# Attention with residual layer norm, one core: a second high-part copy moved to another round, the first input and the query weights loaded in pieces

## What is computed

```
q, k, v = x @ Wq.T, x @ Wk.T, x @ Wv.T + bv
a = softmax(q k.T * 384**-0.5 + adj)        # per graph and head; rows that are all 0 give 0
o = (a @ v) @ Wo.T + bo
out = layernorm(x + o)
```

## Time and profile before

| | |
|---|---|
| median of 3 runs | 1248.02 us (1247.92 to 1248.37) |
| profiled execution | 1248.19 us, its span 1246.4 us |
| TensorE matmul (PE) | 1218.8 us busy, 98% |
| TensorE weight load (PEld) | 1057.3 us, 85% |
| VectorE (DVE) | 1054.4 us, 85% |
| ScalarE (ACT) | 1017.0 us, 82% |
| GpSimd (POOL) | 866.7 us, 70% |

### The profile page before, as it was taken

One profiled execution on the slowest core, in us unless ns is written; L12 is line 12 of the kernel. 1 busy time (PEld: TensorE's weight loads), 2 busy tenths in 40 slices (PEclk: granted clock), 3 DMA queues, 4 the chain that ended last, 5 costly groups with the idle time before them and its releaser, 6 DMA issues.

```text
span 1246.4 us, 34374 instructions
## 1 busy us (share of the span) xinstructions
PE 1218.8 (98%) x11796; PEld 1057.3 (85%) x11796; DVE 1054.4 (85%) x5094; ACT 1017.0 (82%) x4007; POOL 866.7 (70%) x775
## 2 busy tenths in 40 slices
PE   8999999999999999999999999999999999999996
PEld 7888888888888888888888888888888888888885
DVE  5788888888888888888888888888888888888986
ACT  6888888888888878888887888788888888887874
POOL 1777777677677777777776777677777767776774
PEclk9999999999999999999999999999999999999999
DMA  6022211222121222112221212221122212122100
GB/s 232 22 72 86 79 55 54 82 75 80 56 77 61 72 86 80 54 54 83 74 79 61 80 55 71 86 79 54 58 83 71 80 62 79 54 71 86 54 28 26
DMA packets 58895, 88.85 MB, mean 71 GB/s; under 512 B 3680, under 2 KB 54624, under 8 KB 58720
## 3 DMA queue, kind: packets, MB, share of 16 engines
q1 hardware_dynamic: 58720, 86.65, 21.4%
HBM read 61.47 MB, written 25.17 MB: 70 GB/s over the span
## 4 chain that ended last, share of the span: by engine, by line
PE 77%; ACT 19%; DVE 2%; issue 1%; POOL 1%; DMA 0%; POOLq 0%; SPq 0%; DVEq 0%
PE turn_bank L208 17%; PE turn_bank L210 17%; PE turn_bank L209 17%; PE pT_bank L256 12%; ACT probs L496 11%; PE score_bank L244 9%; PE turn_bank L268 6%; ACT pT L503 4%; ACT qkT L484 2%; ACT xT_hi L472 1%; DVE neg_a L624 0%; DVE out_sb L688 0%; DMA xT_raw<-xT_dram 0%; POOL inv_std L779 0%; POOL probs L772 0%
## 5 line engine op out<-in xcount | busy, mean ns | idle before, releaser
L496 ACT ACTIVATE probs<-neg_a,neg_max 128x128 f32<-128x128 f32 x1536 | 596.1, 397 | 3.7 <-DVE neg_max L624 3.5
L772 POOL TENSOR_TENSOR probs<-probs,row_scale 128x768 f32<-128x768 f32 x256 | 376.7, 1471 | 199.8 <-DVE row_scale L652 199.8
L765 POOL TENSOR_TENSOR fold<-neg_a 128x384 f32<-128x384 f32 x256 | 282.9, 1105 | 124.5 <-DVE neg_max L624 124.4
L624 DVE CUSTOM_DVE_ANT_0 neg_a<-score_bank,adj_sb 128x128 f32<-128x128 f32 x1536 | 333.4, 287 | 0.1
L503 ACT ACTIVATE pT<-pT_bank 128x384 f32<-128x384 f32 x512 | 220.7, 484 | 102.9 <-PE pT_bank L256 102.8
L496 ACT ACTIVATION_READ_ACCUMULATOR probs<-neg_a,neg_max 128x1 f32 x1536 | 302.5, 197 | 0.0
L208 PE MATMUL turn_bank<-xT_hi,w_hi 128*128 128x512 f32 (+1 forms) x594 | 240.9, 406 | 2.3 <-DVE w_lo L606 2.3
L210 PE MATMUL turn_bank<-xT_hi,w_lo 128*128 128x512 f32 (+1 forms) x594 | 231.7, 390 | 0.0
L209 PE MATMUL turn_bank<-xT_lo,w_hi 128*128 128x512 f32 (+1 forms) x594 | 230.6, 388 | 0.0
L256 PE MATMUL pT_bank<-ident,probs 128*128 128x128 f32 x1536 | 217.1, 278 | 0.3 <-ACT pT L503 0.3
L256 PEld LDWEIGHTS pT_bank<-ident,probs 128*128 128x128 f32 x1536 | 173.8, 141 | 21.1 <-issue 1.1
(11 more groups left out here) (39 smaller groups left out, 1961.9 us busy)
## 6 DMA issues: line engine op xcount, KB each, us to landing
xT_raw<-xT_dram SPq DMA_DIRECT2D x32, 768.0 KB, 4.7
x_sb<-x_dram SPq DMA_DIRECT2D x32, 768.0 KB, 4.7
out_dram<-out_sb SPq DMA_DIRECT2D x128, 192.0 KB, 1.9
adj_sb<-adj_dram SPq DMA_DIRECT2D x32, 256.0 KB, 3.2
w_raw<-wq_t_dram SPq DMA_DIRECT2D x1, 576.0 KB, 5.7
w_raw<-wk_t_dram SPq DMA_DIRECT2D x1, 576.0 KB, 6.8
w_raw<-wv_t_dram SPq DMA_DIRECT2D x1, 576.0 KB, 7.8
w_raw<-wo_t_dram SPq DMA_DIRECT2D x1, 576.0 KB, 8.4
```

Of the source, the lines that this page charges most:

```text
L496: last = nc.scalar.activation(probs[t % 2][:, u, :], neg_a[t % 2][:, u, :], ACT.Exp, bias=neg_max[t % 2][:, u:u + 1], scale=-1.0, accum_ou ...
L624: last = nc.vector.tensor_tensor_reduce(out=neg_a[t % 2][:, u, :], in0=score_bank[trio][:, c * N:(c + 1) * N], in1=adj_sb[q % 2][:, b, :], ...
L765: nc.gpsimd.tensor_tensor(fold[:, u, :], neg_a[t % 2][:, u, 0:N // 2], neg_a[t % 2][:, u, N // 2:N], ALU.add).then_inc(fold_done, 1)
L772: nc.gpsimd.tensor_tensor(probs[t % 2][:, u, :], probs[t % 2][:, u, :], row_scale[:, u].unsqueeze(2).broadcast_to([P, HALF, N]), ALU.mult) ...
```

## The change

Four things, on three engines.

1. On SyncE the first quad's input comes in three transfers, one per chunk (256 KB each), each with a semaphore of its own (`first_loaded`), and the query weights in three transfers, one per strip of 128 columns (192 KB each, 384 runs of 512 bytes), in the order chunk 0, strip 0, chunks 1 and 2, strips 1 and 2. The other loads follow as before.
2. ScalarE and VectorE split strip 0 right behind chunk 0, then chunks 1 and 2, then the rest.
3. TensorE transposes the identity 24 times, and block 0 of quad 0 goes through `project_first`, which waits for each chunk of `xT_lo` just ahead of that chunk's three matmuls.
4. In ScalarE's `graph` the `xT_hi` copy of chunk 1 for quad q + 2 stands in round 0 behind that of chunk 0, and no longer in round 1. It applies to the 30 quads that have a quad q + 2.

```diff
--- before.py
+++ after.py
@@ -33,7 +33,7 @@
 HALF = HEADS // 2
 SCALE = float(HIDDEN) ** -0.5
 EPS = 1e-5
-WARM_UP = 30
+WARM_UP = 24
 BIG = 3.0e38
 LN_STEPS = 3
 ATTEND_BANK = (0, 1, 1, 0)
@@ -114,7 +114,8 @@
         turn_bank = [bank(f"turn_bank{i}") for i in range(2)]
 
 
-        w_loaded = [sem(f"w_loaded_{name}") for name in "qkvo"]
+        w_loaded = [sem(f"w_loaded{part}") for part in range(len(W_PARTS))]
+        first_loaded = [sem(f"first_loaded{c}") for c in range(CHUNKS)]
         b_loaded = sem("b_loaded")
         xT_loaded = sem("xT_loaded")
         x_loaded = [sem(f"x_loaded{p}") for p in range(2)]
@@ -167,10 +168,23 @@
                 sp.dma_start(xT_raw[:, :, :], xT[bass.ds(q, 1), :, :, :]
                              .rearrange("q p c t -> p (q c) t")).then_inc(xT_loaded, 16)
 
-            load_xT(0)
-            for i, w in enumerate((wq_t, wk_t, wv_t, wo_t)):
-                sp.dma_start(w_raw[:, :, i * HIDDEN:(i + 1) * HIDDEN],
-                             w.rearrange("(c p) o -> p c o", p=P)).then_inc(w_loaded[i], 16)
+            def load_first(c):
+                sp.dma_start(xT_raw[:, c, :], xT[0:1, :, c, :].rearrange("q p t -> p (q t)"))\
+                  .then_inc(first_loaded[c], 16)
+
+            def load_wq(k):
+                sp.dma_start(w_raw[:, :, k * P:(k + 1) * P],
+                             wq_t[:, k * P:(k + 1) * P].rearrange("(c p) o -> p c o", p=P)).then_inc(w_loaded[k], 16)
+
+            load_first(0)
+            load_wq(0)
+            load_first(1)
+            load_first(2)
+            load_wq(1)
+            load_wq(2)
+            for i, w in enumerate((wk_t, wv_t, wo_t)):
+                sp.dma_start(w_raw[:, :, (i + 1) * HIDDEN:(i + 2) * HIDDEN],
+                             w.rearrange("(c p) o -> p c o", p=P)).then_inc(w_loaded[CHUNKS + i], 16)
             for vec, tile in ((bv, bv_sb), (bo, bo_sb)):
                 sp.dma_start(tile[:, :], vec.rearrange("(a f) -> a f", a=1).broadcast_to([P, HIDDEN]))\
                   .then_inc(b_loaded, 16)
@@ -281,6 +295,18 @@
 
                 pe.wait_ge(y_read, t + 2)
 
+            def project_first():
+
+                dst, cols = turn_bank[0][:, :], slice(0, P)
+                pe.wait_ge(w_lo_done, 1)
+                for c in range(CHUNKS):
+                    pe.wait_ge(xT_lo_done, c + 1)
+                    nc.tensor.matmul(dst, w_hi[:, c, cols], xT_hi[0][:, c, :], start=(c == 0), stop=False)
+                    nc.tensor.matmul(dst, w_hi[:, c, cols], xT_lo[0][:, c, :], start=False, stop=False)
+                    last = nc.tensor.matmul(dst, w_lo[:, c, cols], xT_hi[0][:, c, :], start=False,
+                                            stop=(c == CHUNKS - 1))
+                last.then_inc(qk_psum, 1)
+
             def first_half(q):
                 t, kn, ka = QUAD * q, QK * (q + 1), QK * (q + 2)
 
@@ -435,8 +461,8 @@
             pe.wait_ge(ident_steps, 2)
             for _ in range(WARM_UP):
                 nc.tensor.transpose(turn_bank[0][:, 0:P], ident[:, :], ident[:, :])
-            pe.wait_ge(xT_lo_done, CHUNKS)
-            for k in range(QK):
+            project_first()
+            for k in range(1, QK):
                 if k <= CHUNKS:
                     pe.wait_ge(w_lo_done, k + 1)
                 if k >= 2:
@@ -468,13 +494,16 @@
         def _(act):
             def keep_xT_hi(q, c):
 
-                act.wait_ge(xT_loaded, 16 * q + 16)
+                if q == 0:
+                    act.wait_ge(first_loaded[c], 16)
+                else:
+                    act.wait_ge(xT_loaded, 16 * q)
                 nc.scalar.activation(xT_hi[q % 2][:, c, :], xT_raw[:, c, :], ACT.Copy).then_inc(xT_hi_done, 1)
 
             def keep_w_hi(part):
 
                 cols, factor = W_PARTS[part]
-                act.wait_ge(w_loaded[cols.start // HIDDEN], 16)
+                act.wait_ge(w_loaded[part], 16)
                 nc.scalar.activation(w_hi[:, :, cols], w_raw[:, :, cols], ACT.Copy, scale=factor)\
                     .then_inc(w_hi_done, 1)
 
@@ -536,8 +565,6 @@
                     keep_qk(LAST, 0, turn)
                 if t == TAIL + 5:
                     keep_qk(LAST, 4, turn)
-                if b == 1 and has_after:
-                    keep_xT_hi(q + 2, 1)
                 if more2:
                     exp_trio(t + 2, 2)
                 if more:
@@ -548,6 +575,7 @@
                 if b == 0 and has_after:
                     act.wait_ge(v_psum, t + 4)
                     keep_xT_hi(q + 2, 0)
+                    keep_xT_hi(q + 2, 1)
                 if b == 1 and not tail:
                     keep_qk(q + 1, 5, turn)
                 if b == 3 and not tail:
@@ -564,9 +592,11 @@
                     keep_xT_hi(q + 2, 2)
 
 
-            for c in range(CHUNKS):
-                keep_xT_hi(0, c)
-            for part in range(4):
+            keep_xT_hi(0, 0)
+            keep_w_hi(0)
+            keep_xT_hi(0, 1)
+            keep_xT_hi(0, 2)
+            for part in range(1, 4):
                 keep_w_hi(part)
             for k in range(QK):
                 keep_qk(0, k, k % 2)
@@ -727,9 +757,11 @@
 
 
             dve.sem_inc(y_read, 1)
-            for c in range(CHUNKS):
-                keep_xT_lo(0, c)
-            for part in range(len(W_PARTS)):
+            keep_xT_lo(0, 0)
+            keep_w_lo(0)
+            keep_xT_lo(0, 1)
+            keep_xT_lo(0, 2)
+            for part in range(1, len(W_PARTS)):
                 keep_w_lo(part)
             for c in range(CHUNKS):
                 keep_xT_lo(1, c)
```

## The result

The changed kernel takes **1243.72 us** (median of six runs, 1242.13 to 1245.72) against 1247.88 us for the kernel before in the same session (six runs, 1247.74 to 1248.37): ratio 0.9963, interval 0.9952 to 0.9973. It is faster by 4.2 us where 9.2 were forecast, and lies 0.5 us above the upper end of the range. The six runs fall in two groups, three from 1242.13 to 1242.33 (mean granted TensorE clock 0.998) and three from 1245.11 to 1245.72 (0.994 to 0.996). The profiled execution is of the second group: 1245.17 us, span 1243.4.

What follows compares the result with a forecast made beforehand. TensorE, its matmuls busy 98% of the span, was taken as the bound. 8.7 us from the moved copy plus 0.5 from the start gave 9.2 off 1248.19, 1239.0, then 1238.8 us for the median; range 1237.0 to 1243.2.

Steps and rivals of the forecast that it cites:

- The moved copy, 0.29 us per quad, by a margin of 0.04 us: Round 2: block 5's copy comes earlier, so the scores stop waiting for it; 0.29 us in each of 30 quads, 8.7 us.
- The rival that halved this gain: Steady quads: the scores still wait half as long, leaving 4.35 us of gain, 1243.2 us; chance 0.12.
- What is late next is nothing: TensorE's own row: Steady quads: with the scores' wait gone, no other engine holds TensorE, so the whole 0.29 us per quad is kept.
- stays off the path: VectorE follows the quad's 0.29 us shortening out of its 0.55 us idle time in round 3, with 0.26 us remaining.
- Round 0, cost 0: ScalarE in round 0: the added 0.52 us copy cuts idle time from 1.03 to 0.51 us and nobody waits.
- The split of the input and block 0 at 6.1: Start: chunk 0 lands at 4.2 us, its split ends near 6.0, and block 0 starts at 6.1 instead of 8.75.
- The warm-up: TensorE's start: six fewer transposes at 0.165 us each end it at 5.5 instead of 6.5 us; gain 0.
- The strips, 0.4 us for all that is queued behind: Start: query weights in 512-byte runs move at 314 instead of 393 GB/s, delaying later transfers, quad 1's input too, by 0.4 us.
- The gate at quad 1's input, 2.19 us ahead of the first scores: Start: ScalarE waits for that transfer, and the chain from its landing to the first scores takes 2.19 us.
- the 22.3 that the prediction had named as a sign of being wrong: Start: first scores were forecast near 21.7 us; beginning after 22.3 would show the prediction wrong.
- The start costs: Rival: TensorE's idle stretch before the first scores lowers its clock, costing 1.7 us, 1240.5 us; chance 0.15 shared with the end gaining.

Runs made afterwards that it cites:

- e1: The kernel before with only the xT_hi copy of chunk 1 moved from round 1 to round 0: 1243.48 us, ratio 0.9951 to the kernel before.
- e9: The kernel before with the chunk 1 copy moved and VectorE's low-part subtractions of chunks 0 and 1 one place earlier: 1239.75 us, ratio 0.9927 to before.
- e3: The changed kernel with the query weights in one transfer behind chunk 0 instead of three strips: 1242.61 us, ratio 0.9945 to the kernel before.
- e12: The changed kernel with the six transfers reordered, all three input chunks first, then the three strips: 1244.15 us, ratio 0.9958 to the kernel before.
- e4: The changed kernel with ScalarE's copies of quad 1's input behind all six block copies and VectorE's low parts behind graph 0's bias: 1245.18 us, ratio 0.9969 to before.
- e11: The kernel before with the chunk 1 copy moved, input in one transfer, query weights in three strips behind it: 1242.68 us, ratio 0.9949 to before.
- e8: The changed kernel with the query weights in three transfers of 128 rows, the first split waiting for all three: 1246.92 us, ratio 0.9981 to before.
- e2: The changed kernel with the chunk 1 copy put back into round 1, so only the start differs from before: 1249.25 us, ratio 1.0004 to before.
- e6: The changed kernel with quad 1's input issued ahead of the biases and the adjacency: 1241.95 us, ratio 0.9948 to the kernel before.

## Why the prediction was wrong

- *The moved copy, 0.29 us per quad, by a margin of 0.04 us:* right. The scores begin 0.79 us behind attention, and the wait is gone. The rival that halved this gain did not come about; that its 1243.2 us lie close to the median is chance.
- *"What is late next is nothing: TensorE's own row", and VectorE "stays off the path":* this step failed. Next is the v projection of round 2, which waits for VectorE's v evacuation; 0.09 us of the 0.29 are given back in each quad, and nearly all in the thirtieth, 3.0 us in all. 8.7 us became 5.7 (e1: 5.9), and e9 brings back 9.0. I had looked for VectorE's slack in round 3, where it sits idle 0.55 us (after: 0.36), and had not followed its row from round 1 to round 2. Its only idle time is 0.44 us for GpSimd's power, and that power was itself held up by VectorE's own subtraction (e9). So the row did not move up with TensorE: 518.31 - 518.05 = 0.26 us was the room, 0.29 were needed, and the release takes a little as well.
- *Round 0, cost 0:* right, 1.03 to 0.50 us of idle time, and nobody late.
- *The split of the input and block 0 at 6.1:* right; chunk 0 at 3.77, block 0 at 6.23. The warm-up was off: its 24 transposes took 4.95 us where 30 had taken 4.96 (and 4.37 in e3, 5.17 in e12), so 0.165 us each was no constant. It ran right up to the first matmul, whose operands were ready at 5.60, so it may have set that matmul's start. Nothing later hangs on it, since block 2 waits for the copy behind the key weights.
- *The strips, 0.4 us for all that is queued behind:* mis-sized, and the cause wrong. It is 1.6 us at the key weights (10.34 against 8.71; 1.3 in e4, 1.96 in e11) and 0.8 to 1.8 us at quad 1's input. I had read the price off the length of the runs, 314 against 393 GB/s; e8, with runs of 1536 bytes, has the key weights just as late. The Trainium skill ("DMA: Bandwidth & Descriptors", Specifications) has transfers of 512 bytes at line rate. For the weights, e8 gives no sign against that rule. The adjacency's 314 GB/s stay unexplained, and they were not the price of the strips.
- *The gate at quad 1's input, 2.19 us ahead of the first scores:* right (2.17 us; 2.18 in e2 and e3), and e6 shows the gate by taking it away. With this right and the landing 1.4 us later than forecast (20.95 against 19.54), the scores come at 23.12 instead of 21.73, beyond the 22.3 that the prediction had named as a sign of being wrong.
- *"The start costs", given 0.15 with the gain of the quads kept at 8.7:* its mechanism did occur in the profiled execution, 1.46 us for 1.7 reckoned. It was priced on top of a start that gained 0.5 us, and the start gained nothing. It does not by itself part the six runs into 1242.2 and 1245.3, 3.0 us apart. The profiled run, of the slower group, has a second fall at the end, which makes the last nine matmuls 1.2 us longer. The two together are 2.7 us, so falls of the clock may be the whole difference, and the mean clocks (0.998; 0.994 to 0.996) point that way. No run of the faster group was profiled, so this is not shown.

The sum as it came out is 5.7 us (quads) less 0.84 (later scores): 4.9 us, and less 1.46 where the clock falls at the start: 3.4. The median, 4.2 us, lies between, but no run does: the two groups gain 5.6 and 2.7 us. e2, at 1.0004, and e1, at 0.9951, say the same: all the gain is the moved copy's.

## What to carry to other kernels

When a wait of the bounding engine is removed, take the next engine that it waits for and follow that engine's row back to what last held it up. If that does not move up with the bounding engine, the room is the distance from its release to the waiter's start, here 0.26 us for a shift of 0.29. The row may pass through a third engine, as here through GpSimd's power, and the cure may lie there. Splitting a transfer at the head of a queue is to be priced at the last transfer behind it that somebody waits for, not at the first piece, and reordering the queue by who waits (e6) brought the first scores further forward than the split did. An idle stretch of the bounding engine can carry a second price besides its length, here some 1.5 us where the clock fell behind it.
